# A transformer block of attention and a three-layer network on one core: the input normalisation moved from GpSimd to VectorE, with new places in the planner's tables

## The chip, the cores and the metric

The kernel runs on one core of one Trainium2 chip. The metric is the device time of one execution, in microseconds (us); lower is better. Kernels that are to be compared run on the same chip, one after the other.

## What is computed

For 16 sequences of 512 tokens with 256 features, the rows of x are normalised to mean 0 and variance 1 (xn). The output is x + attention(xn) + network(xn).

```python
xn = (x - mean(x)) / sqrt(var(x) + 1e-5)
q, k, v = xn @ wq, xn @ wk, xn @ wv         # 8 heads of 128
q, k = rope(q), rope(k)
s = q @ k.T / 128, masked to the lower triangle
attention = softmax(s) @ v @ wo             # back to 256 features
h = relu(s0 * [xn, -xn] @ sign(k0)) * 2     # 512 -> 1024
h = relu(s1 * h @ sign(k1)) * 2             # 1024 -> 1024
network = s2 * h @ sign(k2)                 # 1024 -> 256
```

All inputs are float32, except k0, k1 and k2, which are booleans read as +1 and -1.

## The kernel before

**Number format.** A float32 value is held as two float16 parts, hi and lo. ScalarE writes hi = round(value), VectorE (in two places GpSimd) writes lo = value - hi, and a product of two such values is three TensorE products (hi hi, hi lo, lo hi). The signs of the network fit in 8 bits, so those products need two.

**Engines.** Five instruction lists (TensorE, VectorE, ScalarE, GpSimd and SyncE, which issues all transfers) are written out ahead by a Python planner and joined by semaphores. Each engine works through its own list in order.

**Loops.** There are 16 sequences (`b`) of 8 heads, 128 heads (`g`) in all. The main loop (L1152) makes one slot for each head. Slot g issues on TensorE: q and k of head g+2 (`qk`, 12 matmuls of 512 columns), then fillers, the scores of head g+1 (`scores`, 12 matmuls), fillers, softmax times v of head g-1 (`values`, 18 matmuls), fillers. Fillers are v, layer 0, layer 1 (made as seven products of halves, `strassen`, names with `seg`), layer 2 and the output projection. The table `PLACES` (L53) says for each filler in which slot of its sequence it goes and in which of the three thirds (order // 2). Slot 1 of a sequence holds both halves of the projection of the sequence before, slot 7 holds only one v.

**What happens to a head.** q and k (L608 to L641): ScalarE copies the two halves of the bank swapped (L612, L613), VectorE multiplies the bank by cos (L617), GpSimd the copy by sin (L621), VectorE adds them (L625), ScalarE takes hi (L631), VectorE lo (L635). Scores (L658 to L714): VectorE adds the mask and takes the row maximum (L666), ScalarE scales it (L674) and takes exp of four tiles (L680), VectorE inverts the sum (L685, L687), GpSimd makes hi (L697), VectorE lo (L703), SyncE transposes both by two transfers (L714), and `values` reads them. A head costs about 16 VectorE instructions.

**The planner's clock.** `clock` counts TensorE work, 1.0 for a matmul of 512 columns. After an operation is issued, each step of its follow-up is put in a list with a due time: the clock plus a number of the table `DELAY` (for the first three heads `EARLY`, for the last two `LATE`; the weights and the first sequence go by `SETUP`). `run_due` (L458) issues what is due, in order of due time, so these numbers fix only the order of instructions on each engine. `need` (L462) issues a step early if something that is being issued reads its result.

**Banks.** Each `Fill` (L472) takes the PSUM bank that the planner expects to be free first: the clock at its end plus a number of `HELD`. TensorE waits there for the real readers of that bank.

**The normalisation.** At the end of slot 3 of each sequence (L1174), `normal(b + 1)` issues `norm` for the next one: on VectorE bn_stats, bn_aggr and the variance (L302 to L307), on GpSimd the power -0.5 (L309). `norm_apply` (L311) comes 20 clock units later and makes xn = (x - mean) * rstd with four instructions of 128 x 256 (L319): for sequence 0 on VectorE, for the others on GpSimd. `norm_T` (L570) then takes hi of all of xn on ScalarE (L577, due after `x_hi`), lo on GpSimd (L581, `x_lo`) and one transposing transfer from SyncE (L585, `x_turned`). Its result xT is first read by the v filler of the next sequence at slot 5, right after slot 5's q and k (`v0`: (-3, 1)). Sequence 1 is normalised in the setup, at the clock time `x1`.

```python
q = pool if b else dve                       # L313
q.wait(done["rstd", b])
...                                          # and for the readers of the old xT
for t in range(4):                           # L318
    ... q.put(lambda e, t=t: e.tensor_scalar(xn(b)[:, t, :], X[:, r, t, :], MV[...], RS[...], subtract, mult))
```

Of the kernel before, what the change touches and what calls it, by code (L numbers as in the profile page):

```python
# [27 lines left out]
T = 512  # L28
# [22 lines left out]


PLACES = {  # L53
# [20 lines left out]
    "seg": ((2, 2), (2, 3), (3, 2), (3, 3), (3, 3), (4, 0), (4, 2), (5, 4)),  # L74
    "seg_15": ((2, 0), (3, 4), (4, 1), (4, 2), (5, 2), (5, 4), (5, 5), (6, 5)),
    "l2_0": ((2, 3), (4, 4)),
    "l2": ((6, 3), (8, 3)),
    "l2_15": ((8, 2), (7, 0)),
    "proj": ((9, 0), (9, 3)),
}  # L80


SETUP = dict(v_max=96.7, o_max=51.6, a11=46.8, a12=45.5, a22=71.6, s1a=1.2, s1b=18.9, s2a=4.8, s2b=11.7, s3a=4.9,
             s3b=1.6, s4a=73.7, s4b=89.9, k2=59.9, x1=129.6, wq1=87.8, wk1=113.9, wq2=87.4, wk2=120.1, wq3=107.7,
             wk3=131.5, wv0=120, wv1=92.1, pads=108.1, ascale=156.1, wo0=146.2, wo1=152.5)
FIRST = ("am0", "l1", "p0", "l1", "qk", "qk", "qk", "am2", "l1", "qk", "p2", "l1", "S", "qk", "S", "l1", "qk", "l1",
         "v", "v", "v", "v")


EARLY = dict(qhi=(23.8, 21.1, 24.7), qlo=(22.9, 20.4, 17.8), bias=(6.3, 7.5, 7.4), exp=(7.3, 2.6, 5.3),  # L90
             inv=(14.5, 0, 10.9), high=(2.7, 14.3, 15.5), low=(20.6, 36.1, 24.1), turned=(42.8, 23.7, 43.6),
             rotated=(13.8, 15.3, 11.9))
LAST = ((-1, range(0, 5)), (0, range(5, 7)), (1, range(7, 8)))


DELAY = dict(hi=0, lo=11.3, swap=0, straight=9.6, crossed=0, rotated=15.5, qhi=21.8, qhi_w=0, qlo=19.8, bias=8.1,
             exp=11.6, exp_i=1.4, differ=4.7, keep_hi=0, keep_lo=17.4, t_hi=10.6, t_lo=18.1, add=7, inv=23.5,
             high=22.6, high_i=6.1, low=43.7, low_i=8.3, turned=66.6, x_hi=48.8, x_lo=60.5, x_turned=70.7)


HELD = dict(am=0, p2=23.2, T=30.9, qk=30.5, S=8.2, PV=23.0, v=13.7, l0=25.3, l1=18.3, seg=21.5, l2=18.6, proj=8.7)


LATE = dict(rotated=14.1, qhi=19.3, qlo=22.0, bias=4.9, exp=11.3, inv=19.6, high=36.1, low=33.0, turned=46.4)


class Queue:
# [28 lines left out]
def block_kernel(nc, x, wq, wk, wv, wo, k0, k1, k2, s3, cosT, sinT, out):  # L136
    ctx = ExitStack()
    with ctx:
# [3 lines left out]
        def sem(name):  # L142
            return ctx.enter_context(nc.semaphore(name))
# [55 lines left out]
        def xn(b):  # L199
            if b == 0:  # L200
                return RT[:, 0:4]
            return XT[:, b % 2].rearrange("p s t c n -> p (s t c n)").bitcast(F32).rearrange("p (t m) -> p t m", t=4)
# [13 lines left out]
        pe, dve, act, pool = (Queue(sem("s_" + n)) for n in ("pe", "dve", "act", "pool"))  # L216
# [93 lines left out]

        def norm_apply(b):  # L311
            r = b % 2
            q = pool if b else dve  # L313
            q.wait(done["rstd", b])
            if b >= 2:
                q.wait(done["qk", 8 * b - 9, 1], *[done["v", b - 2, grp, t] for grp in range(2) for t in range(4)],
                       *[done["l0", b - 2, n] for n in range(8)])
            for t in range(4):  # L318
                done["xn", b] = done["xn", b, t] = q.put(lambda e, t=t: e.tensor_scalar(  # L319
                    xn(b)[:, t, :], X[:, r, t, :], MV[:, r, t, 0:1], RS[:, r, t:t + 1], ALU.subtract, ALU.mult))  # L320
# [127 lines left out]
        def delay(name, g):  # L448

            if g < 3 and name in EARLY:  # L450
                return EARLY[name][g]
            return LATE[name] if g >= G - 2 and name in LATE else DELAY[name]

# [18 lines left out]
        class Fill:  # L472
# [42 lines left out]
            def end(self, read_by):  # L515
                self.mark(self.key)
                users[self.bank] = read_by
                filled[self.bank] = self.seeded or self.columns == 512
                released[self.bank] = clock[0] + HELD[self.key[0]]

# [4 lines left out]
        def split(f, hi_out, lo_out, hi_key, lo_key, scale=1.0, relu=False, free=(), cols=(0, 512), after=None,  # L525
# [11 lines left out]
            def lo():  # L537
# [4 lines left out]
                else:  # L542
                    done[lo_key] = dve.put(lambda e: e.scalar_tensor_tensor(lo_out, src, scale, hi_out, ALU.mult,  # L543
                                                                            ALU.subtract))
            at(DELAY["hi"] + late, hi)
            at(DELAY["lo"] + late, lo)

# [5 lines left out]
        def first_T():  # L553
# [11 lines left out]
            for c, f in enumerate(fs):  # L565
                split(f, XT[:, 0, HI, :, c, :], XT[:, 0, LO, :, c, :], ("xT_hi", c), ("xT", 0, c))
                if c == 0:
                    at(DELAY["hi"], lambda: sign_k0(0))

        def norm_T(b):  # L570
# [12 lines left out]
            def turned():  # L583
# [3 lines left out]
                    s_xt, 16 * b)  # L587
            at(DELAY["x_hi"], hi)
            at(DELAY["x_lo"], lo)
            at(DELAY["x_turned"], turned)  # L590
# [274 lines left out]
        seg = {}  # L865
# [187 lines left out]
        def setup(time, fn, *keys):  # L1053

            item = (SETUP[time] if time in SETUP else time, fn)
            later.append(item)
# [175 lines left out]
```

How the kernel before makes its waits and increments, by code:

```python
    def wait(self, *events):  # L113
        for sem, value in events:
            if self.seen.get(id(sem), 0) < value:
                self.seen[id(sem)] = value
                self.items.append(lambda e, s=sem, v=value: e.wait_ge(s, v))
# [1 line left out]
    def put(self, make, signal=True):  # L119
        if not signal:
            self.items.append(make)
            return None
        self.count += 1
        self.items.append(lambda e: make(e).then_inc(self.sem, 1))
        return (self.sem, self.count)
# [1 line left out]
    def dma(self, make, sem, value):  # L127
        self.items.append(lambda e: make(e).then_inc(sem, 16))
        return (sem, value)
```

## Time and profile before

| | |
|---|---|
| median of 3 runs | 1774.95 us (1774.15 to 1775.36) |
| the profiled execution's own time | 1775.91 us |
| its span (first to last instruction) | 1774.1 us |
| TensorE busy | 1718.2 us (97%), 12720 matmuls |
| VectorE busy | 1534.4 us (86%), 3630 instructions |
| ScalarE busy | 1267.5 us (71%) |
| GpSimd busy | 925.6 us (52%) |
| mean granted TensorE clock | 0.998 |

In the rows, PE is TensorE (PEld its weight loads), DVE VectorE, ACT ScalarE, POOL GpSimd and SPq the transfer queue. All matmuls have the line of one helper (L489), so they are told apart by their operands. The span leaves out 1.8 us of the execution's own time, which lie before the first and after the last instruction. The profile's times of matmuls overlap (a matmul of 512 columns shows 0.38 us and they start 0.22 us apart), so a TensorE that waits a little can still be shown as busy.

### The profile page before, as it was taken

How to read it: one execution, taken by the hardware profiler on the slowest of the kernel's cores; microseconds unless marked ns; L12 is line 12 of the kernel's file. 1: busy time of each engine (PE TensorE's matmuls, PEld its weight loads, DVE VectorE, ACT ScalarE, POOL GpSimd, SP SyncE). 2: the span in 40 equal slices, each digit the busy share in tenths (PEclk: the TensorE clock that was granted, in tenths of full speed). 3: DMA queues.
4: the chain of work that ended last, by engine and by line, in shares of the span. 5: the costliest groups of instructions: out<-in, count | busy, mean ns of one | idle time of the engine just before them, and what ended most of it. 6: DMA issues, size and time to landing. Idle time of an engine off the chain costs nothing.

```text
span 1774.1 us, 34030 instructions
## 1 busy us (share of the span) xinstructions
PE 1718.2 (97%) x12720; PEld 1194.3 (67%) x12720; DVE 1534.4 (86%) x3630; ACT 1267.5 (71%) x2717; POOL 925.6 (52%) x952
## 2 busy tenths in 40 slices
PE   6899989999999999999999999999999999999999
PEld 2356757767676676767767677676766767677667
DVE  8899888897988979888897988979889798888985
ACT  6677676776867677677776867768677776777763
POOL 6555545554545555465455555555456454655632
PEclk9999999999999999999999999999999999999999
DMA  5234543344343434334244333433434344433443
GB/s 172 48 54 73 93 69 78 66 79 81 57 96 60 84 66 71 79 67 91 53 85 83 64 81 67 78 76 63 91 60 88 67 66 85 67 86 58 79 74 69
DMA packets 454838, 134.08 MB, mean 76 GB/s; under 512 B 434704, under 2 KB 453648, under 8 KB 454672
## 3 DMA queue, kind: packets, MB, share of 16 engines
q1 hardware_dynamic: 454672, 131.90, 39.9%
q8 instruction: 100, 1.64, 0.4%
q14 instruction: 66, 0.54, 0.1%
HBM read 14.94 MB, written 8.39 MB: 13 GB/s over the span
## 4 chain that ended last, share of the span: by engine, by line
PE 67%; DVE 19%; ACT 5%; DMA 3%; POOL 3%; issue 2%; SPq 0%; DVEq 0%; POOLq 0%; ACTq 0%
PE bank L489 67%; DVE ph L703 3%; DVE p L666 3%; DVE bank L625 3%; DVE bank L617 2%; DVE qk L635 2%; DMA pt<-ph 2%; ACT p L680 2%; DVE rt L841 1%; POOL xT L319 1%; DVE v L543 1%; DMA xT<-rt 1%; POOL tb L621 1%; DVE hb L822 1%; DVE o L543 1%
## 5 line engine op out<-in xcount | busy, mean ns | idle before, releaser
L697 POOL TENSOR_SCALAR ph<-p,ri 128x384 f16<-128x384 f32 (+3 forms) x512 | 313.2, 612 | 453.9 <-DVE rk L687 416.7
L621 POOL TENSOR_TENSOR tb<-tb,sin 128x512 f32<-128x512 f32 x256 | 331.3, 1295 | 245.2 <-ACT tb L613 238.8
L489 PE MATMUL bank<-hb,wa 128*128 128x256 f16 x3360 | 379.9, 273 | 0.3 <-ACT bank L882 0.3
L489 PEld LDWEIGHTS bank<-hb,wa 128*128 128x128 fp8e5 x3360 | 327.9, 98 | 41.8 <-ACT bank L882 0.5
L680 ACT ACTIVATE p<-p,nm,sc 128x512 f32<-128x512 f32 (+3 forms) x512 | 328.6, 645 | 1.6
L703 DVE SCALAR_TENSOR_TENSOR ph<-p,rk,ph 128x512 f16<-128x512 f32 (+3 forms) x512 | 311.4, 616 | 0.7 <-POOL ph L697 0.7
L666 DVE CUSTOM_DVE_ANT_0 p<-bank,mask 128x512 f32<-128x512 f32 (+3 forms) x512 | 228.9, 484 | 49.9 <-PE bank L489 46.8
L489 PE MATMUL bank<-pt,v 128*128 128x256 f16 (+1 forms) x2304 | 233.1, 256 | 15.1 <-DMA pt<-ph 13.5
L489 PE MATMUL bank<-qk 128*128 128x512 f16 (+3 forms) x1536 | 229.9, 299 | 16.0 <-DVE qk L635 14.6
L489 PEld LDWEIGHTS bank<-pt,v 128*128 128x128 f16 x2304 | 202.6, 98 | 43.0 <-DMA pt<-ph 20.2
L489 PEld LDWEIGHTS bank<-qk 128*128 128x128 f16 x1536 | 132.8, 98 | 121.4 <-DVE qk L635 22.4
L631 ACT ACTIVATE qk<-bank 128x512 f16<-128x512 f32 x256 | 151.0, 590 | 80.0 <-DVE bank L625 79.5
L635 DVE TENSOR_TENSOR qk<-bank,qk 128x512 f16<-128x512 f32 x256 | 174.3, 682 | 29.5 <-ACT qk L631 28.3
L625 DVE TENSOR_TENSOR bank<-bank,tb 128x512 f32<-128x512 f32 x256 | 177.3, 693 | 18.2 <-POOL tb L621 13.2
L612 ACT ACTIVATE tb<-bank 64x512 f32<-64x512 f32 x256 | 151.9, 593 | 50.4 <-PE bank L489 43.0
L489 PE MATMUL bank<-xT,wk 128*128 128x512 f16 x768 | 186.7, 379 | 1.2 <-DVE wk L365 1.0
L489 PE MATMUL bank<-wv,xT 128*128 128x512 f16 x768 | 183.7, 379 | 3.5 <-DMA xT<-rt 3.5
L489 PE MATMUL bank<-xT,wq 128*128 128x512 f16 x768 | 186.7, 379 | 0.1
L617 DVE TENSOR_TENSOR bank<-bank,cos 128x512 f32<-128x512 f32 x256 | 176.7, 690 | 4.8 <-ACT tb L613 4.6
L489 PE MATMUL bank<-wo,o 128*128 128x256 f16 x1536 | 172.9, 273 | 0.0
L851 POOL TENSOR_TENSOR hb<-rt,hb 128x1024 f16<-128x1024 f32 x60 | 132.4, 2206 | 62.1 <-ACT hb L847 60.8
L489 PEld LDWEIGHTS bank<-wo,o 128*128 128x128 f16 x1536 | 150.2, 98 | 20.6
(107 smaller groups left out, 2259.2 us busy)
## 6 DMA issues: line engine op xcount, KB each, us to landing
out<-xnat SPq DMA_DIRECT2D x32, 256.0 KB, 2.4
xnat<-in_x SPq DMA_DIRECT2D x15, 512.0 KB, 3.8
pt<-ph SPq DMA_TRANSPOSE x256, 4.3
o<-in_k SPq DMA_DIRECT2D x1, 1024.0 KB, 7.2
v<-in_wq SPq DMA_DIRECT2D x1, 1024.0 KB, 9.2
v<-in_wk SPq DMA_DIRECT2D x1, 1024.0 KB, 10.9
ph<-in_wv SPq DMA_DIRECT2D x1, 1024.0 KB, 13.5
o<-in_wo SPq DMA_DIRECT2D x1, 1024.0 KB, 10.2
```

What stands on the lines that cost most here:

```text
L489: self.todo.append(lambda e, stop=False: e.matmul(self.ps[:, cols[0]:cols[1]], lhsT, rhs, start=first, stop=stop, skip_group_check=skip))
L612: act.put(lambda e: e.activation(TB[0:64, r, :], f.ps[64:128, :], ACT.Copy))
L617: done["straight", n] = dve.put(lambda e: e.tensor_tensor(f.ps[:, :], f.ps[:, :], COS[:], ALU.mult))
L621: done["crossed", n] = pool.put(lambda e: e.tensor_tensor(tb, tb, SIN[:], ALU.mult))
L625: done["rot", n] = dve.put(lambda e: e.tensor_tensor(f.ps[:, :], f.ps[:, :], tb, ALU.add))
L631: done["qk_hi", n] = act.put(lambda e: e.activation(hi, f.ps[:, :], ACT.Copy))
L635: done["qk_lo", n] = dve.put(lambda e: e.tensor_tensor(lo, f.ps[:, :], hi, ALU.subtract))
L666: done["max", g, i] = dve.put(lambda e, i=i, a=a, w=w: e.tensor_tensor_reduce(out=P[:, r, S_OFF[i]:S_OFF[i] + w], in0=f.ps[:, a:a + w], in ...
L680: done["exp", g, i] = act.put(lambda e: e.activation(v, v, ACT.Exp, bias=NM[:, g % 4, i:i + 1], scale=SC[:, 0:1], accum_out=SM[:, g % 4, i ...
L697: done["P_hi", g, i] = pool.put(lambda e: e.tensor_scalar(part(r, i, HI), v, RI[:, g % 4, i:i + 1], 4096.0, ALU.mult, ALU.mult))
L703: done["P_lo", g, i] = dve.put(lambda e: e.scalar_tensor_tensor(part(r, i, LO), v, RK[:, g % 4, i:i + 1], part(r, i, HI), ALU.mult, ALU.su ...
L851: done["h0t", b, i] = pool.put(lambda e: e.tensor_tensor(HB[:, 3:7, LO, i, :], RT[:, 4:8], HB[:, 3:7, HI, i, :], ALU.subtract))
```

## The change

`norm_apply` puts its four instructions on VectorE for every sequence. The tables `PLACES`, `SETUP`, `EARLY`, `DELAY`, `HELD` and `LATE` get new numbers. Everything else is the same: the same instructions in the same number, apart from the engine of these 60.

```diff
@@ -51,57 +51,57 @@
 
 
 PLACES = {
-    "l1_2": ((5, 2),),
-    "l1_3": ((7, 1),),
-    "l1_4": ((2, 2),),
-    "l1_5": ((0, 5),),
+    "l1_2": ((6, 3),),
+    "l1_3": ((8, 0),),
+    "l1_4": ((3, 4),),
+    "l1_5": ((-1, 0),),
     "l1_6": ((1, 2),),
-    "l1_7": ((1, 4),),
-    "v_0": ((6, 5),),
-    "v_1": ((-1, 5),),
-    "v_2": ((0, 0),),
-    "v_3": ((1, 2),),
+    "l1_7": ((1, 5),),
+    "v_0": ((7, 0),),
+    "v_1": ((-1, 0),),
+    "v_2": ((-1, 2),),
+    "v_3": ((6, 4),),
     "v_4": ((4, 1),),
     "v_5": ((2, 5),),
-    "v_6": ((2, 4),),
-    "v_7": ((3, 3),),
+    "v_6": ((2, 5),),
+    "v_7": ((3, 2),),
     "l0_1": ((2, 2), (3, 0), (3, 5), (5, 2)),
     "l0": ((-2, 4), (0, 2), (0, 5), (1, 1)),
     "v0_1": ((-4, 4), (-3, 5), (-2, 3), (-2, 2)),
-    "v0": ((-3, 5), (-3, 1), (-1, 0), (0, 4)),
-    "v1": ((3, 5), (4, 1), (4, 0), (1, 4)),
+    "v0": ((-3, 5), (-3, 1), (-1, 1), (0, 4)),
+    "v1": ((3, 5), (4, 1), (4, 0), (2, 5)),
     "seg_1": ((-1, 2), (-1, 3), (0, 5), (2, 5), (3, 3), (4, 0), (4, 1), (4, 2)),
     "seg": ((2, 2), (2, 3), (3, 2), (3, 3), (3, 3), (4, 0), (4, 2), (5, 4)),
-    "seg_15": ((2, 0), (3, 4), (4, 1), (4, 2), (5, 2), (5, 4), (5, 5), (6, 5)),
+    "seg_15": ((2, 0), (4, 0), (4, 1), (4, 2), (5, 2), (5, 4), (5, 5), (6, 5)),
     "l2_0": ((2, 3), (4, 4)),
-    "l2": ((6, 3), (8, 3)),
-    "l2_15": ((8, 2), (7, 0)),
+    "l2": ((6, 2), (8, 3)),
+    "l2_15": ((8, 2), (7, 2)),
     "proj": ((9, 0), (9, 3)),
 }
 
 
-SETUP = dict(v_max=96.7, o_max=51.6, a11=46.8, a12=45.5, a22=71.6, s1a=1.2, s1b=18.9, s2a=4.8, s2b=11.7, s3a=4.9,
-             s3b=1.6, s4a=73.7, s4b=89.9, k2=59.9, x1=129.6, wq1=87.8, wk1=113.9, wq2=87.4, wk2=120.1, wq3=107.7,
-             wk3=131.5, wv0=120, wv1=92.1, pads=108.1, ascale=156.1, wo0=146.2, wo1=152.5)
+SETUP = dict(v_max=86.8, o_max=51.1, a11=46.2, a12=45.4, a22=72, s1a=1.3, s1b=31.3, s2a=1.7, s2b=11.9, s3a=5.4,
+             s3b=1.6, s4a=73.7, s4b=97.5, k2=59.5, x1=130.9, wq1=88, wk1=115.4, wq2=88.2, wk2=124.8, wq3=107,
+             wk3=132.4, wv0=117.8, wv1=92, pads=111.2, ascale=146, wo0=146.9, wo1=154.7)
 FIRST = ("am0", "l1", "p0", "l1", "qk", "qk", "qk", "am2", "l1", "qk", "p2", "l1", "S", "qk", "S", "l1", "qk", "l1",
          "v", "v", "v", "v")
 
 
-EARLY = dict(qhi=(23.8, 21.1, 24.7), qlo=(22.9, 20.4, 17.8), bias=(6.3, 7.5, 7.4), exp=(7.3, 2.6, 5.3),
-             inv=(14.5, 0, 10.9), high=(2.7, 14.3, 15.5), low=(20.6, 36.1, 24.1), turned=(42.8, 23.7, 43.6),
-             rotated=(13.8, 15.3, 11.9))
+EARLY = dict(qhi=(23.8, 21.1, 24.7), qlo=(24.7, 20.4, 17.8), bias=(8.4, 7.5, 7.1), exp=(2.8, 2.6, 6.5),
+             inv=(15.6, 0.4, 10.9), high=(2.7, 14.3, 15.2), low=(19.9, 36.1, 24.5), turned=(38.0, 23.0, 38.4),
+             rotated=(14.5, 15.3, 11.9))
 LAST = ((-1, range(0, 5)), (0, range(5, 7)), (1, range(7, 8)))
 
 
-DELAY = dict(hi=0, lo=11.3, swap=0, straight=9.6, crossed=0, rotated=15.5, qhi=21.8, qhi_w=0, qlo=19.8, bias=8.1,
-             exp=11.6, exp_i=1.4, differ=4.7, keep_hi=0, keep_lo=17.4, t_hi=10.6, t_lo=18.1, add=7, inv=23.5,
-             high=22.6, high_i=6.1, low=43.7, low_i=8.3, turned=66.6, x_hi=48.8, x_lo=60.5, x_turned=70.7)
-
-
-HELD = dict(am=0, p2=23.2, T=30.9, qk=30.5, S=8.2, PV=23.0, v=13.7, l0=25.3, l1=18.3, seg=21.5, l2=18.6, proj=8.7)
-
-
-LATE = dict(rotated=14.1, qhi=19.3, qlo=22.0, bias=4.9, exp=11.3, inv=19.6, high=36.1, low=33.0, turned=46.4)
+DELAY = dict(hi=0, lo=11.8, swap=0, straight=9.6, crossed=0, rotated=15.5, qhi=21.8, qhi_w=0, qlo=19.8, bias=8.1,
+             exp=11.6, exp_i=1.4, differ=4.7, keep_hi=3.9, keep_lo=16.1, t_hi=11.4, t_lo=17.5, add=8, inv=23.5,
+             high=23.1, high_i=6.2, low=43.7, low_i=8.5, turned=66.1, x_hi=39.4, x_lo=60, x_turned=66.5)
+
+
+HELD = dict(am=0, p2=13.6, T=33.4, qk=29.1, S=4.8, PV=18.4, v=19.1, l0=28.4, l1=18.3, seg=23.8, l2=18.8, proj=9.8)
+
+
+LATE = dict(rotated=14.4, qhi=21.8, qlo=22.0, bias=6.2, exp=10.4, inv=8.3, high=33.5, low=36.9, turned=46.5)
 
 
 class Queue:
@@ -310,7 +310,7 @@
 
         def norm_apply(b):
             r = b % 2
-            q = pool if b else dve
+            q = dve
             q.wait(done["rstd", b])
             if b >= 2:
                 q.wait(done["qk", 8 * b - 9, 1], *[done["v", b - 2, grp, t] for grp in range(2) for t in range(4)],
```

## Rows read from the trace of the kernel before

**Rows 1.** Waits of TensorE, whole span: us in total, times, longest us.
```profile
PE bank L489 <- DVE qk L635: 14.6, 15, 3.0
PE bank L489 <- DMA pt<-ph: 13.5, 19, 3.5
...
PE bank L489 <- DMA xT<-rt: 3.5, 3, 1.3
```

**Rows 2.** Windows of four sequences: PE, PEld, DVE, ACT, POOL busy, PEclk, DMA share, GB/s.
```profile
237.00:348.30 111.30, 107.03 (x791) 74.83 (x789) 94.71 (x226) 78.33 (x170) 56.41 (x59) 0.98 0.41 73
780.20:887.80 107.60, 106.45 (x802) 75.07 (x801) 94.25 (x226) 78.40 (x170) 57.11 (x58) 1.00 0.37 74
456.00:565.00 109.00, 106.58 (x802) 74.95 (x801) 94.30 (x226) 78.14 (x170) 57.12 (x59) 1.00 0.39 73
1211.20:1320.00 108.80, 106.87 (x803) 74.95 (x801) 94.41 (x226) 78.41 (x170) 56.57 (x59) 1.00 0.41 74
```

**Rows 3.** Chain of waits through one sequence: start us, us, what.
```profile
780.14 0.69 DVE p L666
...
799.02 88.68 PE bank L489 x673
887.73 0.69 DVE p L666
```

**Rows 4.** TensorE's timeline, five starts and the waits before them.
```profile
793.81 1.82 PE L489 MATMUL bank<-pt,v 128*128 128x256 f16 x18 [0.34 <-DMA pt<-ph]
799.02 1.79 PE L489 MATMUL bank<-qk 128*128 128x512 f16 x12 [0.81 <-DVE qk L635]
...
858.65 1.46 PE L489 MATMUL bank<-xT,wq 128*128 128x512 f16 x6
859.95 1.46 PE L489 MATMUL bank<-xT,wk 128*128 128x512 f16 x6
...
876.68 1.46 PE L489 MATMUL bank<-wv,xT 128*128 128x512 f16 x6
```

**Rows 5.** GpSimd and the transfer queue, the same sequence's normalisation.
```profile
859.72 1.03 POOL L309 TENSOR_TENSOR rs<-ve,half 128x4 f32<-128x4 f32 x1 [2.42 <-DVE ve L307]
...
863.98 4.82 POOL L319 TENSOR_SCALAR xT<-xnat,mv,rs 128x256 f32<-128x256 f32 x4
869.98 2.13 POOL L581 TENSOR_TENSOR rt<-xT,rt 128x1024 f16<-128x1024 f32 x1 [1.17 <-ACT rt L577]
...
872.13 1.81 SPq L585 DMA_TRANSPOSE xT<-rt  x1
```

**Rows 6.** Line L585: time from issue to landing, all 15.
```profile
DMA to landing us min/median/max: 4.3/4.3/5.9
```

**Rows 7.** Groups by line and shape, whole span: busy us, mean ns.
```profile
L319 DVE TENSOR_SCALAR rt<-xnat,mv,rs 128x256 f32<-128x256 f32 x4 | 1.4, 409 | 0.9 <-POOL rs L309 0.9
L302 DVE BATCH_NORM_STATS2 bn<-xnat 128x6 f32<-128x256 f32 x64 | 22.4, 408 | 3.6 <-DMA xnat<-in_x 3.5
```

**Rows 8.** VectorE's timeline after the normalisation: first and last idle gap.
```profile
862.73 0.70 DVE L625 TENSOR_TENSOR bank<-bank,tb 128x512 f32<-128x512 f32 x1 [0.65 <-POOL tb L621]
...
868.17 0.69 DVE L666 CUSTOM_DVE_ANT_0 p<-bank,mask 128x512 f32<-128x512 f32 x1 [0.83 <-PE bank L489]
...
874.41 0.18 DVE L685 RECIPROCAL ri<-sm 128x4 f32<-128x4 f32 x1 [1.06 <-ACT p L680]
```

**Rows 9.** Setup, GpSimd and VectorE: the normalisation of sequence 1.
```profile
65.97 5.82 POOL L319 TENSOR_SCALAR xT<-xnat,mv,rs 128x256 f32<-128x256 f32 x4
...
74.63 0.70 DVE L625 TENSOR_TENSOR bank<-bank,tb 128x512 f32<-128x512 f32 x1 [2.98 <-POOL tb L621]
```

**Rows 10.** Setup, TensorE's timeline: the two waits behind it.
```profile
77.20 1.48 PE L489 MATMUL bank<-qk 128*128 128x512 f16 x9 [2.59 <-DVE qk L635]
79.73 0.50 PE L489 MATMUL bank<-qk 128*128 128x256 f16 x3 [1.05 <-DVE v L543]
```

**Rows 11.** TensorE's timeline near the end: a late start.
```profile
1707.35 1.82 PE L489 MATMUL bank<-pt,v 128*128 128x256 f16 x18 [1.04 <-DMA pt<-ph]
```


## The prediction

> **What bounds the kernel now.** I read TensorE's waits first, since it is busy 97% of the span. Its waits for q and k sum to 14.6 us, those for transposed softmax to 13.5 and those for xT to 3.5 [rows 1]. These are all that a better order could win back, besides waits that hide in overlapping matmuls. Then I compared sequences. An ordinary one takes 107.6 us with 106.45 us of TensorE busy, so 1.15 us idle; the two with an xT wait take 109.0 and 108.8, and the one from 237 us takes 111.3 at a mean clock of 0.98 [rows 2]. The chain of waits shows what kind of time this is: 88.68 us of pure TensorE, then from 780.14 to 799.02 almost only VectorE [rows 3]. Those 18.9 us are slots 6, 7 and the start of 0, where a slot has little TensorE work but a whole head for VectorE. Both idle gaps of the sequence are there, 0.34 and 0.81 us [rows 4]. So the kernel is bound by TensorE for five sixths and by VectorE for one sixth of each sequence. GpSimd, which the change relieves, appears only in the path to xT and in the setup.
>
> **One: xT comes earlier.** First the unit: q and k of a head start 858.65 and 859.95, six matmuls of 512 columns in 1.30 us, so a planner unit is 0.217 us [rows 4]. Now GpSimd starts xn at 863.98 and needs 4.82 us. ScalarE's hi adds 1.17 us of waiting and GpSimd's lo 2.13 us. The transfer is issued at 872.13 [rows 5]. It lands 4.3 us later, at worst 5.9 [rows 6]. That is 876.4 or 878.0, and v would start at 876.68 [rows 4]. The usual margin is thus 0.25 us, and the worst landing is 1.3 us late. That is the size of the three xT waits, 3.5 us together [rows 1].
>
> After the change xn costs four instructions of 0.41 us, 1.64 us [rows 7]. They fall due 20 units after slot 4 begins, at 863.0. The power is ready at 859.72 + 1.03 = 860.75 [rows 5], so VectorE's list should not stand still for it, and xn is complete at 864.7. The 9.4 units off x_hi bring ScalarE's hi to 39.4 units, 867.2. With the same 1.17 and 2.13 us the transfer goes out at 870.5; x_turned (66.5 units) leaves it first in SyncE's list. It lands at 874.8, at worst 876.4: the margin is 1.9 us, or 0.3. All three waits go. By the windows they cost 109.0 - 107.6 = 1.4 and 108.8 - 107.6 = 1.2 us [rows 2], and 1.3 for the third, whose sequence I can't compare cleanly. **Gain 3.9 us**, bounds 0 (no margin won, should VectorE be late) and 3.9.
>
> **Two: 1.64 us more on VectorE in each of 15 sequences, 24.6 us.** It lands in slot 4, where TensorE has 71 units of work. Between 862.73 and 874.41 VectorE has six idle gaps, from 0.65 to 1.06 us, which sum to 4.0 [rows 8]. The first already absorb the 1.64, before the VectorE-bound stretch begins at 877. Queued behind xn are the add and lo of q and k of head g+2, which no score reads before the next slot. **Cost 0.** If that cover were gone it would be the whole 24.6 us, the upper bound; the lower is a gain of 1 us, as GpSimd is free for the sin product for which VectorE waits 0.65 us there.
>
> Here the Trainium skill speaks against the change. What the row shows: the four VectorE instructions take 409 ns each, as long as bn_stats over the same 256 elements (408) [rows 7], so nothing in them runs at double rate. The Trainium skill (SBUF — State Buffer, "Who interferes with whom") says that `tensor_scalar` on SBUF operands can enter a two-port mode and then holds the port pair that it shares with GpSimd, which "fully blocks"; by that rule GpSimd would stand still through these instructions. The row speaks against the mode, and I give that case a rival below.
>
> **Three: the setup.** For sequence 1 xn is in GpSimd's list ahead of a sin product. It takes 5.82 us, and VectorE stands 2.98 us before the add at 74.63 [rows 9]. The chain leads on to the late scores, 2.59 us for q and k and 1.05 us for a bank that a v still holds [rows 10]. Without it GpSimd is ready, but VectorE has 1.64 us more work ahead of that add: 2.98 - 1.64 = 1.3 us earlier. The 1.05 us is a matter of `HELD`: v's banks are now expected back after 19.1 units in place of 13.7, those of the scores after 4.8 in place of 8.2, so the next scores should take other banks. I take half of it, 0.5. **Gain 1.8 us**, bounds -1.6 (VectorE's work in the path, no relief) and 3.6 (both waits). The other new `SETUP` times mostly keep the order: v_max is pulled by `need` at its reader in both tables, and s1b is pulled ahead of s2b.
>
> **Four: the places.** l2 (6, 3) to (6, 2) and v0's third tile (-1, 0) to (-1, 1) stay in the same third with nothing to change places with: 0. v1's last tile (six matmuls, 6 units or 1.3 us) goes from slot 1 (89 units, the longest) to the end of slot 2; `values` needs it in slot 5: 0 either way. The moves for sequence 15 and `LATE` touch the last 80 us, where the largest gap is 1.04 us [rows 11]. `inv` at 8.3 units stands earlier in VectorE's list than ScalarE's exp can be done, so VectorE waits, with lo of the last q and k behind it; the scores that read these come a whole slot later. I take 0, bounds -1.0 and 3 (one of VectorE's longer waits in the setup, 2.98, as the nearest row).
>
> **Five: the hand-overs.** Sorted by due time, nearly all new delays leave VectorE's order in slots 6 and 7 alone: keep_lo 16.1, the last lo of a v 29.8 and the low parts 8.5 apart cross nothing before the lo of q and k at 31.8. Hence I expect the 1.15 us per sequence to remain. On ScalarE keep_hi (3.9) falls behind the row bias, one hi and one exp in slot 0, where TensorE is ahead of its readers. **0**, bounds a gain of 14 x 1.15 = 16 us (the stretch fits) and a loss of 14 x 0.7 = 10 us (one more instruction of 0.7 us, the size of an add [rows 8], in each stretch).
>
> **Sum.** -3.9 - 1.8 = -5.7 us. The profiled execution took 1775.91 us (span 1774.1), 1.0 above the median. 1775.9 - 5.7 = 1770.2, and against the median 1774.95 - 5.7 = **1769.3 us**, which I predict.
>
> **Rivals.** *The gains don't reach the end:* TensorE starts earlier, and the transposed softmax becomes the next thing late. For it: the longest wait for such a transfer is 3.5 us [rows 1], in the slow sequence that follows the first xT wait. Against: the ordinary sequences show 0.34 us there [rows 4]. Half of 3.9 and nothing of the setup gives 1773.0. *The VectorE stretch fits:* if bank choice and order remove most of the two gaps, half of 16 us comes on top: 1761. For it: nearly all `HELD` numbers are new, and I can't follow which bank is picked. Against: the stretch is full of VectorE work that the change does not reduce. *The VectorE stretch grows (slower):* a bank whose reader is late makes TensorE wait in slot 7, before the scores, and VectorE starts its next maxima that much later. The price is 0.7 us in 14 sequences, 10 us, less the 3.9: 1781. It decides from 0.4 us per sequence upward. *xn holds GpSimd up (slower):* by the row unlikely. If GpSimd stood still for 1.64 us and the cover failed, 15 x 1.64 = 24.6 us, less the setup and xT gains of which none would be left: 1799. The rule of the Trainium skill's SBUF page stands behind this one. *The change doesn't do what it says* has no room: the engine is named in one line.
>
> **Chances.** About 0.2% (3.5 us) is what a measurement of this kernel can tell from no change. Forecast 0.45, gains lost 0.27, stretch fits 0.15, stretch grows 0.10, GpSimd held up 0.03. Faster is the forecast and the fitting stretch, 0.60; same 0.27; slower 0.13. The forecast alone spans 1766 to 1771.4; with the fitting stretch and the lost gains the range is 1761 to 1777, which leaves out the slower cases and the full 16 us.
>
> **What the profile would show.** Right: 64 instructions of L319 on VectorE at 0.41 us; the first xT transfers issued about 1.6 us earlier against slot 4; no TensorE wait for xT; VectorE's gaps in slot 4 smaller; ordinary sequences still 107.6 us with the 0.81 us wait for q and k; the wait at 77.20 shorter by 1.3. Wrong: ordinary sequences that differ from 107.6 by more than 0.3 us, or L319 or its GpSimd neighbours longer than 1.3 us, or a new wait of TensorE for a VectorE lo of v or of the scores' maxima.

## The result, and the profile after

| | before | after |
|---|---|---|
| median of the runs | 1775.15 us (1774.15 to 1775.62) | 1786.38 us (1784.47 to 1788.38) |
| profiled execution: own time, span | 1775.91, 1774.1 us | 1785.74, 1784.0 us |

The change makes the kernel slower: ratio 1.0064, 95% interval 1.0047 to 1.0082. The forecast was 1769.3 us, with a range that ended at 1777. Two of the prediction's signs of being wrong are there: ordinary sequences are 1.1 us longer, and instructions of L319 take up to 1.37 us. The rest of this section reads where 9.9 us of span came from.

First the page of the kernel after: busy time by engine, then two of its costliest groups (busy us, mean ns, idle time before them and what ended most of it).

```profile
PE 1721.4 (96%) x12720; PEld 1194.4 (67%) x12720; DVE 1601.3 (90%) x3690; ACT 1267.3 (71%) x2717; POOL 844.9 (47%) x892
...
L703 DVE SCALAR_TENSOR_TENSOR ph<-p,rk,ph 128x512 f16<-128x512 f32 (+3 forms) x512 | 354.6, 702 | 11.3 <-POOL ph L697 11.3
...
L489 PE MATMUL bank<-wo,o 128*128 128x256 f16 x1536 | 173.1, 273 | 13.0 <-DVE qk L635 13.0
```

The page of the kernel before, for the first two; its `wo,o` has no idle time before it:

```profile
PE 1718.2 (97%) x12720; PEld 1194.3 (67%) x12720; DVE 1534.4 (86%) x3630; ACT 1267.5 (71%) x2717; POOL 925.6 (52%) x952
...
L703 DVE SCALAR_TENSOR_TENSOR ph<-p,rk,ph 128x512 f16<-128x512 f32 (+3 forms) x512 | 311.4, 616 | 0.7 <-POOL ph L697 0.7
```

VectorE is busy 67 us more. The moved normalisation explains only part of it (35.7 us for its 60 instructions): L703, the low part of the softmax, which the change does not touch, went from 616 to 702 ns, 43 us over its 512 instructions. And the output projection (`wo,o`) now waits 13.0 us for VectorE.

TensorE's waits of the kernel after (us in total, times, longest), against [rows 1]:

```profile
PE bank L489 <- DVE qk L635: 27.0, 30, 2.2
PE bank L489 <- DMA pt<-ph: 12.9, 18, 2.6
...
PE bank L489 <- DMA xT<-rt: 1.8, 1, 1.8
```

That for q and k grew by 12.4 us, in 15 more places; the other two fell by 0.6 and 1.7. These three make +10.1. All other waits of TensorE together fell by 3.5, to +6.6 in all, and its busy time grew by 3.2 (1718.2 to 1721.4), which makes the 9.9 us of the span but for 0.1. So the xT waits mostly went, as forecast, and the wait for q and k took the gain and far more.

TensorE's timeline shows where. After, slots 0 and 1 of one sequence (idle time before a start in square brackets):

```profile
799.74 1.79 PE L489 MATMUL bank<-qk 128*128 128x512 f16 x12 [0.79 <-DVE qk L635]
...
820.81 1.79 PE L489 MATMUL bank<-qk 128*128 128x512 f16 x12
823.49 5.41 PE L489 MATMUL bank<-wo,o 128*128 128x256 f16 x48 [0.89 <-DVE qk L635]
```

The same place before:

```profile
820.10 1.79 PE L489 MATMUL bank<-qk 128*128 128x512 f16 x12
821.73 5.40 PE L489 MATMUL bank<-wo,o 128*128 128x256 f16 x48
```

The wait of 0.79 in slot 0 is the old one [rows 4]. New is 0.89 us in slot 1, before the second half of the output projection: its bank is one that the lo of q (L635) still reads. It is there once per sequence. The same start comes at 823.49 and at 932.17, so an ordinary sequence takes 108.7 us, where it took 107.6 [rows 2]: 1.1 us. Nearly all of it is at this place: the projection starts 2.68 us after the matmuls of the scores (823.49 - 820.81), where it was 1.63 (821.73 - 820.10), 1.05 us more. Only 0.89 of that shows as a wait, since the shown times of matmuls overlap.

Is the bank another one, or is its reader later? VectorE's own timeline answers. After:

```profile
809.79 1.01 DVE L822 SCALAR_TENSOR_TENSOR hb<-bank,hb 128x512 f16<-128x512 f32 x2
810.72 3.11 DVE L703 SCALAR_TENSOR_TENSOR ph<-p,rk,ph 128x384 f16<-128x384 f32 x3
813.75 0.68 DVE L543 SCALAR_TENSOR_TENSOR o<-bank,o 128x512 f16<-128x512 f32 x1
814.35 1.70 DVE L703 SCALAR_TENSOR_TENSOR ph<-p,rk,ph 128x512 f16<-128x512 f32 x1
...
822.75 1.45 DVE L635 TENSOR_TENSOR qk<-bank,qk 128x512 f16<-128x512 f32 x2
```

Before:

```profile
809.04 0.62 DVE L703 SCALAR_TENSOR_TENSOR ph<-p,rk,ph 128x384 f16<-128x384 f32 x1
809.58 1.01 DVE L822 SCALAR_TENSOR_TENSOR hb<-bank,hb 128x512 f16<-128x512 f32 x2
810.52 2.00 DVE L703 SCALAR_TENSOR_TENSOR ph<-p,rk,ph 128x256 f16<-128x256 f32 x2
812.44 0.68 DVE L543 SCALAR_TENSOR_TENSOR o<-bank,o 128x512 f16<-128x512 f32 x1
813.04 0.73 DVE L703 SCALAR_TENSOR_TENSOR ph<-p,rk,ph 128x512 f16<-128x512 f32 x1
...
820.48 1.44 DVE L635 TENSOR_TENSOR qk<-bank,qk 128x512 f16<-128x512 f32 x2
```

These are the same instructions in another order: the two lo of layer 0's segments (L822, `keep_lo`) have moved ahead of the low part with 384 columns. (A line with x2 or x3 shows the shape of its first instruction: the three low parts have 384, 256 and 128 columns, the two of before 256 and 128.) From the first of them to the lo of q and k it takes 820.48 - 809.04 = 11.44 us before and 822.75 - 809.79 = 12.96 after. GpSimd's timeline shows what stands beside the slow ones. After:

```profile
810.08 2.12 POOL L851 TENSOR_TENSOR hb<-rt,hb 128x1024 f16<-128x1024 f32 x1
812.30 1.85 POOL L697 TENSOR_SCALAR ph<-p,ri 128x384 f16<-128x384 f32 x3
814.23 1.27 POOL L621 TENSOR_TENSOR tb<-tb,sin 128x512 f32<-128x512 f32 x1
```

Before:

```profile
809.34 2.31 POOL L851 TENSOR_TENSOR hb<-rt,hb 128x1024 f16<-128x1024 f32 x1
811.74 2.19 POOL L697 TENSOR_SCALAR ph<-p,ri 128x384 f16<-128x384 f32 x3
814.02 1.27 POOL L621 TENSOR_TENSOR tb<-tb,sin 128x512 f32<-128x512 f32 x1
```

In the kernel before, the 384-column part started 0.30 us ahead of L851 and was done in 0.62 us, and the 512-column part was done (813.77) before L621 began. After the swap the 384-column part stands behind L822 and starts in the middle of L851; everything behind it is later, so the 512-column part starts 0.12 us behind L621 and takes 1.70 in place of 0.73 us. It looks as if such an instruction of VectorE can't run while such a one of GpSimd does. The low part reads p and ph, both in SBUF; L851 and L621 read two SBUF tensors too. L822, which reads one input from a bank, takes 1.01 us in both kernels, though the whole of it ran beside L851 before.

Last, the normalisation itself, L319, which now runs on VectorE. Its 60 instructions, minimum, median and maximum in ns, then VectorE's and GpSimd's timeline of one sequence:

```profile
L319 DVE TENSOR_SCALAR xT<-xnat,mv,rs x60: 396/402/1373, 64.0 to 1628.2; 128x256 f32<-128x256 f32 x60
```

```profile
864.55 2.33 DVE L319 TENSOR_SCALAR xT<-xnat,mv,rs 128x256 f32<-128x256 f32 x4
866.80 0.68 DVE L625 TENSOR_TENSOR bank<-bank,tb 128x512 f32<-128x512 f32 x1
```

```profile
863.21 2.56 POOL L621 TENSOR_TENSOR tb<-tb,sin 128x512 f32<-128x512 f32 x2
```

The median is the 0.41 us forecast. But the first of the four takes about 1.36 us: it starts at 864.55 and ends at 865.91, just behind GpSimd's two products, which end at 865.77. A group of four takes 2.33 us, not 1.64.

### The profile page after: what moved, and what is told of

The parts are those of the page before. It is cut to its first block, busy times and chain, and to the rows that moved or that the text cites. A ratio compares the mean times of both kernels' runs of the same rounds, so it can differ in the third digit from the quotient of the medians.

```text
span 1784.0 us, 34009 instructions
## 1 busy us (share of the span) xinstructions
PE 1721.4 (96%) x12720; PEld 1194.4 (67%) x12720; DVE 1601.3 (90%) x3690; ACT 1267.3 (71%) x2717; POOL 844.9 (47%) x892
## 3 DMA queue, kind: packets, MB, share of 16 engines
q8 instruction: 100, 1.64, 0.4%
## 4 chain that ended last, share of the span: by engine, by line
DVE 40%; PE 40%; ACT 12%; issue 4%; DMA 2%; POOL 2%; SPq 0%; DVEq 0%; POOLq 0%
PE bank L489 40%; DVE ph L703 9%; ACT p L680 7%; DVE bank L625 6%; DVE bank L617 5%; DVE p L666 4%; DVE rt L841 4%; DVE qk L635 3%; DVE hb L822 2%; DMA pt<-ph 2%; DVE v L543 2%; ACT qk L631 1%; DVE o L543 1%; DVE xnat L964 1%; ACT tb L612 1%
## 5 line engine op out<-in xcount | busy, mean ns | idle before, releaser
L697 POOL TENSOR_SCALAR ph<-p,ri 128x256 f16<-128x256 f32 (+3 forms) x512 | 307.5, 601 | 463.9 <-DVE rk L687 426.9
L621 POOL TENSOR_TENSOR tb<-tb,sin 128x512 f32<-128x512 f32 x256 | 332.8, 1301 | 261.2 <-ACT tb L613 252.8
L703 DVE SCALAR_TENSOR_TENSOR ph<-p,rk,ph 128x512 f16<-128x512 f32 (+3 forms) x512 | 354.6, 702 | 11.3 <-POOL ph L697 11.3
L680 ACT ACTIVATE p<-p,nm,sc 128x128 f32<-128x128 f32 (+3 forms) x512 | 328.5, 644 | 1.5
L631 ACT ACTIVATE qk<-bank 128x512 f16<-128x512 f32 x256 | 151.6, 592 | 127.4 <-DVE bank L625 126.5
L635 DVE TENSOR_TENSOR qk<-bank,qk 128x512 f16<-128x512 f32 x256 | 174.9, 683 | 16.8 <-ACT qk L631 14.6
L851 POOL TENSOR_TENSOR hb<-rt,hb 128x1024 f16<-128x1024 f32 x60 | 129.7, 2161 | 61.9 <-ACT hb L847 60.5
```

Source lines behind the costliest of these rows:

```text
L621: done["crossed", n] = pool.put(lambda e: e.tensor_tensor(tb, tb, SIN[:], ALU.mult))
L631: done["qk_hi", n] = act.put(lambda e: e.activation(hi, f.ps[:, :], ACT.Copy))
L635: done["qk_lo", n] = dve.put(lambda e: e.tensor_tensor(lo, f.ps[:, :], hi, ALU.subtract))
L680: done["exp", g, i] = act.put(lambda e: e.activation(v, v, ACT.Exp, bias=NM[:, g % 4, i:i + 1], scale=SC[:, 0:1], accum_out=SM[:, g % 4, i ...
L697: done["P_hi", g, i] = pool.put(lambda e: e.tensor_scalar(part(r, i, HI), v, RI[:, g % 4, i:i + 1], 4096.0, ALU.mult, ALU.mult))
L703: done["P_lo", g, i] = dve.put(lambda e: e.scalar_tensor_tensor(part(r, i, LO), v, RK[:, g % 4, i:i + 1], part(r, i, HI), ALU.mult, ALU.su ...
```

## The experiments

The theory after this reading, **the collision**: `keep_lo` 16.1 puts a low part beside L851; VectorE stands still there and at L621 for some 1.5 us per sequence, and TensorE pays 0.9 to 1.1 of it. The rivals: **the bank** (the new `HELD` gives the projection a bank whose reader is late), and **the load** (VectorE's additional work for xn, 25 to 36 us, no longer fits).

### One place alone, in both directions

The kernel after with one number of before:

```diff
-             exp=11.6, exp_i=1.4, differ=4.7, keep_hi=3.9, keep_lo=16.1, t_hi=11.4, t_lo=17.5, add=8, inv=23.5,
+             exp=11.6, exp_i=1.4, differ=4.7, keep_hi=3.9, keep_lo=17.4, t_hi=11.4, t_lo=17.5, add=8, inv=23.5,
```

> The changed kernel with keep_lo back at 17.4 units: in each sequence one low part of 128 x 384 (L703) goes back ahead of the two lo instructions of layer 0 (L822) in VectorE's list; nothing else differs. Order theory (this swap puts the low part beside GpSimd's 2.1 us instruction L851, VectorE loses about 1.1 us per sequence and TensorE then waits 0.9 us in slot 1 for the lo of q): ordinary sequences come back from 108.7 to about 107.6 us, the wait of TensorE before the second half of the projection is gone, and the time is 1786.4 - 14 x 1.1 = 1771 us, below the kernel before. Engine theory (VectorE has too much work with xn on it): no difference, 1786. Bank theory (HELD): no difference, 1786.

Measured: 1771.32 us, ratio to before 0.9979 (0.9969 to 0.9989). The kernel is 15.1 us faster than after, by one number. TensorE's waits (us, times, longest):

```profile
PE bank L489 <- DVE qk L635: 14.0, 16, 2.2
PE bank L489 <- DMA pt<-ph: 13.8, 18, 3.5
```

The 30 waits for q and k are 16 again, and the projection no longer waits. VectorE's timeline has the order of before back, and with it its durations:

```profile
806.07 0.62 DVE L703 SCALAR_TENSOR_TENSOR ph<-p,rk,ph 128x384 f16<-128x384 f32 x1
806.62 1.01 DVE L822 SCALAR_TENSOR_TENSOR hb<-bank,hb 128x512 f16<-128x512 f32 x2
807.55 2.01 DVE L703 SCALAR_TENSOR_TENSOR ph<-p,rk,ph 128x256 f16<-128x256 f32 x2
```

The kernel before with that number alone:

```diff
-             exp=11.6, exp_i=1.4, differ=4.7, keep_hi=0, keep_lo=17.4, t_hi=10.6, t_lo=18.1, add=7, inv=23.5,
+             exp=11.6, exp_i=1.4, differ=4.7, keep_hi=0, keep_lo=16.1, t_hi=10.6, t_lo=18.1, add=7, inv=23.5,
```

> The kernel before with keep_lo at 16.1 units alone: the same swap in each sequence, xn still on GpSimd and all banks as before. Order theory: VectorE loses 1 to 1.5 us per sequence in slots 0 and 1, TensorE's wait in slot 1 appears at 0.5 to 0.9 us, and the time is 1775.2 + 15 x 0.9 = 1789, at least 1782 us. Engine theory and bank theory: no difference, 1775.

Measured: 1790.69 us, ratio 1.0088 (1.0073 to 1.0103), 15.5 us slower than the 1775.15 of before (16.1 than the 1774.57 that it took beside this run). The same wait is there in TensorE's timeline, with xn still on GpSimd and `HELD` as before:

```profile
827.89 5.41 PE L489 MATMUL bank<-wo,o 128*128 128x256 f16 x48 [0.89 <-DVE qk L635]
```

So neither the load nor the new `HELD` is needed for the loss. Everything else in the change together is worth 1771.32 against 1774.57, a gain of 3.3 us.

### The bank

The kernel after with the whole `HELD` of before:

```diff
-HELD = dict(am=0, p2=13.6, T=33.4, qk=29.1, S=4.8, PV=18.4, v=19.1, l0=28.4, l1=18.3, seg=23.8, l2=18.8, proj=9.8)
+HELD = dict(am=0, p2=23.2, T=30.9, qk=30.5, S=8.2, PV=23.0, v=13.7, l0=25.3, l1=18.3, seg=21.5, l2=18.6, proj=8.7)
```

> The changed kernel with the table HELD of the kernel before: the same instructions in the same order on every engine, only the PSUM banks and TensorE's waits for them differ. Bank theory: a part of the 11 us comes from banks that come free later, and this kernel is 3 to 11 us faster, 1775 to 1783 us. Order theory: the planner picks a bank of the same reader (the lo of q of slot 1) for the second half of the projection in both tables, so the 0.9 us wait stays: 1785 to 1788 us, with at most 1 us for the v bank in the setup.

Measured: 1788.47 us, ratio 1.0076 (1.0061 to 1.0091). The wait stays, 28.1 us in 30 places for q and k, and the kernel is no faster than after. The choice of banks is not the cause.

### Is it the order, or what GpSimd does beside it?

The swap could cost by itself, since two instructions now stand ahead of a low part. To separate the two, GpSimd's L851 was replaced by two memsets of the same tile, one behind the other, which only write. This leaves out the low part of layer 0's differences, so the output has less precision there.

```diff
-                done["h0t", b, i] = pool.put(lambda e: e.tensor_tensor(
-                    HB[:, 3:7, LO, i, :], RT[:, 4:8], HB[:, 3:7, HI, i, :], ALU.subtract))
+                for _ in range(2):
+                    done["h0t", b, i] = pool.put(lambda e: e.memset(HB[:, 3:7, LO, i, :], 0.0))
+                    pool.wait(done["h0t", b, i])
```

In the kernel after:

> The changed kernel (keep_lo 16.1) with GpSimd's subtraction L851, which reads two tensors of SBUF, replaced by two memsets of the same 128 x 1024 elements, one after the other, which only write. (Left out: the lo part of the differences of layer 0, which is set to zero.) Port theory (VectorE's low part L703 has both inputs in SBUF, and stands still while GpSimd works through an instruction that reads SBUF): the low part of 128 x 384 is back at about 0.6 us in slot 0, and the kernel takes 1769 to 1772 us, within 2 us of its twin e6. Order theory without a port (the swap alone puts VectorE's work in a worse place): still 15 us slower than e6, about 1785 us.

And in the kernel with `keep_lo` at 17.4:

> The twin of e5 with keep_lo at 17.4 (kernel e1, with the two memsets in place of L851; the same part is left out). Both theories: near e1, 1767 to 1772 us. It is the base against which e5 is read: the difference e5 - e6 is the price of the swap without GpSimd's reads, against 1786.4 - 1771.3 = 15.1 us with them.

Measured:

| `keep_lo` | L851 reads two tensors | memsets |
|---|---|---|
| 16.1 | 1786.38 us | 1770.21 us |
| 17.4 | 1771.32 us | 1769.99 us |

The right column was measured on another chip, on which the kernel before took 1775.24 us (1774.57 beside the kernel with 17.4 in the left one). The swap costs 15.1 us with the subtraction beside it and 0.2 us with memsets there, which is less than can be told from nothing. VectorE's timeline of the kernel after with memsets, then GpSimd's:

```profile
806.11 1.01 DVE L822 SCALAR_TENSOR_TENSOR hb<-bank,hb 128x512 f16<-128x512 f32 x2
807.04 1.26 DVE L703 SCALAR_TENSOR_TENSOR ph<-p,rk,ph 128x384 f16<-128x384 f32 x3
```

```profile
806.39 1.96 POOL L852 MEMSET hb<- 128x1024 f16 x2
```

GpSimd is busy as long (1.96 us against 2.12) at the same place, and the three low parts take 1.26 us in place of 3.11. Over the whole kernel the 384-column form (form, busy us and mean ns) goes from the first line to the second:

```profile
L703 DVE SCALAR_TENSOR_TENSOR ph<-p,rk,ph 128x384 f16<-128x384 f32 x128 | 110.2, 861 | 0.0
```

```profile
L703 DVE SCALAR_TENSOR_TENSOR ph<-p,rk,ph 128x384 f16<-128x384 f32 x128 | 79.9, 624 | 0.1
```

The Trainium skill has the rule (SBUF — State Buffer, "Who interferes with whom"): "A DVE instruction with two SBUF inputs contends with a GpSimd instruction that reads SBUF, not with one that only writes it", and the later one blocks for the whole of the earlier. All four kernels agree with it. A memset differs from a subtraction in more than its reads, so that the reads are what counts rests on the rule and on one thing more: beside GpSimd's L697, which reads one tensor of SBUF and isn't a subtraction, the low parts of the kernel after are slow too. Of its 3.11 us for three, 1.48 lie before L851 ends at 812.20, and the 1.63 behind it are still more than the 1.26 for all three beside memsets. What the rule doesn't give is the price: 15 us of 1775 come from the place in which the two meet, ahead of a reader whose bank is wanted next.

### xn: which engine, and how it falls

The kernel before, its tables whole, with L319 on VectorE:

```diff
-            q = pool if b else dve
+            q = dve
```

> The kernel before with the four instructions of xn on VectorE for every sequence and all tables as before. Order theory: ordinary sequences stay at 107.6 us, since slot 4 has 4.0 us of idle VectorE; the setup gains 1 to 3 us and the three waits for xT go or stay (x_hi is still at 48.8 units, so ScalarE takes hi at its old place): 1769 to 1774 us. Engine theory: VectorE's added 1.64 us per sequence shows in each sequence as 0.7 to 1.1 us, 1785 to 1790 us.

Measured: 1773.75 us, ratio 0.9995 (0.9985 to 1.0004). The engine alone is worth less than can be told from nothing. The kernel after with the line the other way round, its tables whole:

```diff
-            q = dve
+            q = pool if b else dve
```

> The changed kernel with xn back on GpSimd for sequences 1 to 15, all new tables kept. Order theory: sequences stay at 108.7 us, the setup loses its 3 us and waits for xT may come back: 1786 to 1793 us. Engine theory: VectorE is relieved and sequences come back to 107.6 us: 1772 to 1776 us.

Measured: 1790.83 us, ratio 1.0087 (1.007 to 1.0103). Against after, the move to VectorE is worth 4.5 us, and in the old tables 0.8 (1773.75 against 1774.57), so the new tables suit it. And the wait before `wo,o` is there with xn on GpSimd too (0.90 us at 829.19): once more, not the load.

The long first instruction of each group of xn was then tried by its place. In the kernel with `keep_lo` at 17.4, xn falls due two units later, behind an add and a cos product, when GpSimd's sin products are over:

```diff
-            at(20, lambda: norm_apply(b))
+            at(22, lambda: norm_apply(b))
```

> The kernel after with keep_lo at 17.4 (whose L319 on VectorE has a mean of 653 ns and takes 2.34 us per quartet, the first of the four ending when GpSimd's two sin products L621 end), and the four xn instructions due at 22 units in place of 20, so that an add and a cos product (L625, L617) stand ahead of them on VectorE and GpSimd is done when they start. Theory (a tensor_scalar that reads SBUF stands still while GpSimd's two-tensor product runs): the quartet takes 1.64 us, L319 has a mean near 0.41 us, VectorE's busy time falls by about 10 us (13 to 14 sequences by 0.7), xn is complete about 0.6 us later in its slot. As slot 4 has idle gaps on VectorE, the time stays at 1771.3, within 2 us. Rival (the first of a group is slow by itself, a start or a wait for rs inside it): the quartet stays at 2.3 us and the mean at 650 ns wherever it stands.

Measured: 1771.28 us (1771.32 without the step); L319 has a mean of 420 ns in place of 653, and VectorE is busy 1564.1 us in place of 1576.7. The timelines of VectorE and GpSimd:

```profile
860.02 1.37 DVE L319 TENSOR_SCALAR xT<-xnat,mv,rs 128x256 f32<-128x256 f32 x4
```

```profile
857.48 2.56 POOL L621 TENSOR_TENSOR tb<-tb,sin 128x512 f32<-128x512 f32 x2
```

GpSimd ends at 860.04, xn starts at 860.02, and all four take 1.37 us. So the first isn't slow by itself: it stood still beside GpSimd's product. The 12.6 us that VectorE saves bring nothing, as slot 4 has idle time enough.

### Tries at the wait that was there all along

Four kernels on top of `keep_lo` 17.4 aimed at the 0.8 us in slot 0. The first puts the lo of k earlier everywhere:

```diff
-DELAY = dict(hi=0, lo=11.8, swap=0, straight=9.6, crossed=0, rotated=15.5, qhi=21.8, qhi_w=0, qlo=19.8, bias=8.1,
+DELAY = dict(hi=0, lo=11.8, swap=0, straight=9.6, crossed=0, rotated=15.5, qhi=21.8, qhi_w=-2.9, qlo=19.8, bias=8.1,
```

> Kernel e1 with qhi_w at -2.9: hi and lo of k come 2.9 units earlier, so in slot 7 VectorE makes the lo of k ahead of one low part (0.39 us) and the lo of a v (0.60 us). If VectorE's queue sets the scores of slot 0, the 0.8 us wait of TensorE shrinks by 0.4 to 0.8 us per sequence (VectorE may now wait for ScalarE's hi, 0.6 us): 1760 to 1766 us. Rival: the wait for hi takes the whole gain, or ScalarE's exp come later and the transposed softmax with them: 1771 to 1776 us.

A miss: 1823.98 us, ratio 1.0278. The due time is that of every head, and of the hi on ScalarE too. ScalarE's waits, first with `qhi_w` at 0, then at -2.9:

```profile
ACT qk L631 <- DVE bank L625: 121.2, 167, 4.4
```

```profile
ACT qk L631 <- DVE bank L625: 244.9, 230, 4.5
```

ScalarE now reaches the hi before VectorE's add is done, and its exps queue behind it: VectorE's wait for them went from 66.4 to 134.3 us. The second changes one place per sequence, in slot 7: the lo of v's third tile goes behind the lo of k.

```diff
-            at(DELAY["lo"] + late, lo)
+            at(DELAY["lo"] + late + lo_late, lo)
...
-                  ("vp", b, grp, t, HI), ("vp", b, grp, t, LO), scale=2.0 ** -6, free=free)
+                  ("vp", b, grp, t, HI), ("vp", b, grp, t, LO), scale=2.0 ** -6, free=free, lo_late=4.2 if (grp, t) == (0, 2) and b > 1 else 0)
```

> Kernel e1 with one exchange per sequence in VectorE's list, in slot 7: the lo of the v tile (L543, 0.60 us, nobody waits for it) goes behind the lo of k (L635), for which the scores of slot 0 wait 0.80 us. All other lists are the same. Order theory: that wait shrinks by 0.6 us to 0.2 us in 14 sequences, 1771.3 - 8.4 = 1763 us. Rival (the gain is only moved: VectorE, bound through slots 6, 7 and 0, makes TensorE wait later, or the pair falls beside a GpSimd instruction): 1769 to 1773 us.

Measured: 1767.05 us, ratio 0.9956 (0.9942 to 0.9971), 4.3 us less than before this step, about half of the 8.4 expected. The wait in slot 0 did fall from 0.8 to 0.19 us:

```profile
899.36 1.79 PE L489 MATMUL bank<-qk 128*128 128x512 f16 x12 [0.19 <-DVE qk L635]
```

But a sequence gains less than that: this start is 107.16 us behind the same one of the sequence before (792.20), where without the step it was 107.63 (903.65 - 796.02), 0.47 us in place of 0.61.

The third moves a low part of 256 columns behind it as well:

```diff
-                at(delay("low", g) + n * DELAY["low_i"], lambda i=i: low(i))
+                at(delay("low", g) + n * DELAY["low_i"] + (4.8 if n == 2 and g % 8 == 7 else 0), lambda i=i: low(i))
```

> Kernel e9 with a second exchange in the same place: the low part of 128 x 256 (L703, 0.39 us) also goes behind the lo of k. Order theory: the rest of the wait goes, but VectorE now waits 0.1 to 0.2 us for ScalarE's hi; 1 to 3 us less than e9, 1760 to 1762 us. Rival: the low part belongs to a head whose transposed softmax TensorE reads in slot 0; its transfer starts 0.6 us later and TensorE waits for that, or the low part runs into GpSimd's L851 and stands still: no gain over e9, or 2 to 10 us slower.

Measured: 1766.28 us, ratio 0.9953 (0.9936 to 0.997). The wait in slot 0 is gone, and 0.19 us of the one before the projection are back:

```profile
789.74 1.79 PE L489 MATMUL bank<-qk 128*128 128x512 f16 x12
...
812.80 5.41 PE L489 MATMUL bank<-wo,o 128*128 128x256 f16 x48 [0.19 <-DVE qk L635]
```

0.8 us less than the second is no difference that these runs can tell: the rival's "no gain", and not the 1760 to 1762 expected. The same with xn two units later:

> The same step of xn from 20 to 22 units on the kernel of the run e10 (1766.28 us; keep_lo 17.4, one lo of v and one low part a place later). Theory: VectorE is busy about 10 us less, all of it in slot 4, where it has gaps, so the time stays at 1766.3, within 2 us. Rival (VectorE is short of time in slot 4 after all, and what is late there reaches slot 5 and the scores): the time falls by 3 us or more, to 1763.

Measured: 1767.47 us, ratio 0.9958 (0.9944 to 0.9973): no gain, as with the step alone. So the fastest versions found are the three with the lo of v moved, 1766 to 1768 us: 7 to 8 us under the kernel before and 19 to 20 under the changed one.

## Why the prediction was wrong

**Step Five failed**, where it says that "nearly all new delays leave VectorE's order in slots 6 and 7 alone". That sentence is true and looks at the wrong slots. I sorted the new due times only where VectorE is short of time, and took slot 0 on ScalarE's side alone ("TensorE is ahead of its readers"). In slot 0 `keep_lo` passes the low part of 384 columns: counted in planner units from the slot's start the lo was due at 44.9 and the low part at 44.5 before, and at 43.6 and 44.7 after. One low part changed places with two lo there, which by count of work is worth nothing. What it cost was 1.5 us of standing still on VectorE, because of what GpSimd does at that moment. Slot 0's margin was smaller than I took it to be: it held about 0.5 of the 1.5 us, and the rest reached the bank of the projection in slot 1, where TensorE starts 1.05 us later. 0.89 of that shows as a wait, 13.0 us over the kernel, and `keep_lo` alone is worth 15.1 us of time. Step Five had put it at 0.

The slower rival had the right kind of mechanism, a bank whose reader is late, and two thirds of the price (10 us against 15.1), at the wrong place (slot 7, before the scores). It had a chance of 0.10, and its 1781 lay outside the range. The upper bound of step Five, 14 times 0.7, was for one more instruction; the collision is twice that on VectorE and 1.05 on TensorE.

**Step Two** was right in its result and wrong in its size. The sum said 24.6 us; the group measures 35.7 (60 at 654 ns). The cover in slot 4 held both. Its argument from the skill was wrong: 409 ns, "as long as bn_stats", was read as speaking against any hold on the shared ports. That row stood where GpSimd was idle, and a duration without a neighbour can't show contention. Who stood still was mostly not GpSimd but VectorE, which came second. The Trainium skill's page (SBUF — State Buffer, "Who interferes with whom") says of the two-port modes that who issues first has the ports, and lists `tensor_scalar` as one that can enter them. By the rate these instructions were in no such mode, and still they contended; whether their two scalars in SBUF count as a second input, no run here separates. The reverse case, GpSimd behind xn, shows only in the setup and is small: L697 starts at 64.23, 0.18 us behind an L319, and takes 0.78 us where it takes 0.69 at 809.31.

**Step One** was half right. Three xT waits of 3.5 us became one of 1.8. In the sequence that I followed, the transfer is issued at 873.18, 12.75 us after its slot began at 860.43; before it was 872.13 - 858.65 = 13.48. That is 0.7 us earlier, where I expected 1.6. VectorE's standing still is part of this (2.33 us for a group in place of 1.37), and ScalarE is the rest: its hi waits behind another (L631), which waits 1.98 us for VectorE's add, and that add now stands behind xn. The wait that is left is early, in sequence 2:

```profile
223.46 1.47 PE L489 MATMUL bank<-wv,xT 128*128 128x512 f16 x6 [1.79 <-DMA xT<-rt]
```

There SyncE's list holds the transfer behind two transposes of pt, which end at 217.98: it is issued at 218.03, and lands in 5.4 us where the median is 4.3.

**Step Three** was right in direction, and gave the second wait to the wrong cause. Both waits of [rows 10] shrank, the first by 0.35 us where I expected 1.3:

```profile
74.55 1.48 PE L489 MATMUL bank<-qk 128*128 128x512 f16 x9 [2.24 <-DVE qk L635]
76.41 0.50 PE L489 MATMUL bank<-qk 128*128 128x256 f16 x3 [0.38 <-DVE v L543]
```

The second has nothing to do with `HELD`, for which step Three had 0.5 us. It is as short in the kernel after with the old `HELD`, and as long as before in the kernel with all new tables and xn on GpSimd. First the one, then the other:

```profile
76.73 0.50 PE L489 MATMUL bank<-qk 128*128 128x256 f16 x3 [0.38 <-DVE v L543]
80.57 0.50 PE L489 MATMUL bank<-qk 128*128 128x256 f16 x3 [1.05 <-DVE v L543]
```

The start at 74.55 was at 77.20. At 160.68 TensorE is 3.1 us ahead of the kernel before (163.75), with all of the setup in it, where I expected 1.8. With xn on VectorE in the old tables it is 0.9 ahead there (162.83), so most of the 3.1 needs the new tables; which of their numbers was not tried. From there the 1.1 us per sequence took it back.

**Step Four** was taken as 0, and no run has the places alone. The kernel with `keep_lo` back has them all, and with it the last stretch is as long as before: from q and k in slot 6 of the last sequence but one to the end it takes 1774.1 - 1639.4 = 134.7 us before and 1770.2 - 1635.5 = 134.7 with them. Ordinary sequences are at 107.6 in both.

**The sum.** -5.7 us was forecast for everything but the hand-overs; without the collision the change measures -3.3 (1771.32 against 1774.57). With it, the runs give +11.2.

## What to carry to other kernels

When a change shifts due times, sort the old and new lists of every engine in every slot, not only where time is short, and hold each pair that changes places against what the engine beside it does in those microseconds. For instructions of VectorE with two SBUF inputs the neighbour's operands matter more than their own length: start them just ahead of GpSimd's reads, if GpSimd can afford the wait, or well behind. A stretch has slack only against a delay of the size you tried; a swap of neighbours can make one instruction three times as long (0.62 us to 1.91).

## What the hardware showed that I had not expected

- A low part of 0.62 us (384 columns) or 0.73 us (512 columns) that starts behind GpSimd's L851 (2.12 us) or L621 (1.27 us) takes until that is over, and then about 0.2 us less than its own time: 810.72 to 812.62 with L851's end at 812.21, 814.35 to 816.05 with L621's end at 815.50. Beside memsets of the same place and about the same length it takes no longer than alone.
- It works the other way too. Before, L697's part of 128 columns starts together with the low part of 512 columns and takes 0.90 us; after, the same part starts at the end of the low parts and takes 0.37:

```profile
813.04 0.90 POOL L697 TENSOR_SCALAR ph<-p,ri 128x128 f16<-128x128 f32 x1
813.78 0.37 POOL L697 TENSOR_SCALAR ph<-p,ri 128x128 f16<-128x128 f32 x1
```

- A `tensor_scalar` on VectorE with one SBUF tensor and two SBUF scalars per partition stood still as well: about 1.36 us beside GpSimd's product, 0.40 behind it. It did so though it shows no higher rate: 0.33 us from one start to the next for 256 elements, as bn_stats over the same.
- The cost is not in the total of collisions. The kernel before has them too (2.00 us for two low parts of 256 and 128 columns), and L319's 12.6 us cost nothing. What counts is which instruction stands ahead of a reader whose bank is wanted next.
